# Delta rule: odd heads on exchanged quarters of the rows, solve products on eight array tiles in two banks, per-chunk products ordered over sixteen tiles

## What is computed

```python
def step(S, xs):
    qc, kc, vc, bc = xs
    kb = kc * bc[:, None]
    A = jnp.tril(kb @ kc.T, -1)
    U = solve_triangular(eye + A, vc * bc[:, None] - kb @ S, lower=True)
    o = qc @ S + jnp.tril(qc @ kc.T) @ U
    return (S + kc.T @ U, o)
```

## Time and profile before

| | |
|---|---|
| median of three runs | 824.07 us |
| the profiled execution, span | 869.1 us |
| projecting stage, 17.0 to 113.6 us | 96.6 us, TensorE busy 58.0 |
| delta stage, steps 0 and 1 | 27.0 us, TensorE busy 17.1 |
| delta stage, steps 2 to 15 | 143.6 us, TensorE busy 124.2 |
| all that comes behind 291 us | 578.1 us |

### The profile page before, as it was taken

How to read it: one execution, slowest core, us unless ns; L and a number is a source line. 1 busy time by engine, 2 the same in 40 slices (tenths; PEclk the granted TensorE clock), 3 DMA queues, 4 the chain that set the end, 5 groups by cost and what they waited for, 6 DMA issues and landing times. The chain is left out here.

```text
span 869.1 us, 38511 instructions
## 1 busy us (share of the span) xinstructions
PE 638.0 (73%) x15559; PEld 550.7 (63%) x15559; DVE 388.2 (45%) x1166; ACT 275.3 (32%) x666; POOL 375.3 (43%) x773
## 2 busy tenths in 40 slices
PE   5775457888888585616998368889985269989993
PEld 4564346888888484516988335567664158978992
DVE  3664602222222135661666413445762844456662
ACT  4552211111111121404665133434532023334441
POOL 4574554211110372055888473220100444387675
PEclk9796655555555566856999757889997569999997
DMA  4001231131110470064655110000000556555551
GB/s 124 8 15 32 69 91 40 59 97 49 54 49 34 142 225 1 0 105 144 196 181 171 40 43 23 16 15 4 4 4 2 91 140 203 191 182 184 198 192 38
DMA packets 64818, 75.08 MB, mean 86 GB/s; under 512 B 16048, under 2 KB 42704, under 8 KB 64704
## 3 DMA queue, kind: packets, MB, share of 16 engines
q1 hardware_dynamic: 60384, 64.38, 24.1%
q0 software_dynamic: 4320, 9.18, 4.4%
HBM read 19.83 MB, written 11.24 MB: 36 GB/s over the span
## 5 line engine op out<-in xcount | busy, mean ns | idle before, releaser
L2017 PE MATMUL e_psH<-spare,e_up_w 128*128 x728 | 102.2, 284 | 9.7 <-issue 6.2
L2017 PEld LDWEIGHTS e_psH<-spare,e_up_w 128*128 128x128 f32 x728 | 90.1, 195 | 18.1 <-issue 18.1
L586 POOL TENSOR_TENSOR tb<-tinv,mb 128x128 f32<-128x128 f32 x64 | 24.3, 403 | 116.3 <-PE d_psY L606 110.1
L2082 ACT ACTIVATE e_pre<-e_psH 128x256 f32<-128x256 f32 x91 | 34.6, 382 | 71.1 <-PE e_psH L2017 66.6
L2027 PE MATMUL e_psY<-vb,e_hT 128*128 x364 | 56.0, 276 | 0.2
L1345 ACT ACTIVATE e_hT<-e_psH,e_b 128x128 f32<-128x128 f32 x156 | 44.6, 368 | 27.9 <-PE e_psH L1301 20.1
L2190 DVE SCALAR_TENSOR_TENSOR e_row<-e_psY,e_row 128x128 f32 x91 | 32.0, 351 | 47.9 <-issue 35.8
L1249 POOL DMA_INDIRECT e_row<-xe_dram,e_read_at x39 | 42.8, 1099 | 17.3 <-issue 6.8
L2183 DVE TENSOR_TENSOR e_hT<-e_pre,e_psH 128x256 f32<-128x256 f32 x91 | 37.6, 413 | 25.3 <-ACT e_pre L2082 15.2
L2027 PEld LDWEIGHTS e_psY<-vb,e_hT 128*128 128x128 f32 x364 | 47.9, 192 | 1.0 <-issue 0.9
L1733 DVE TENSOR_TENSOR spare<-l_psA,l_tri 128x512 f32<-128x512 f32 x64 | 39.7, 680 | 14.3 <-PE l_psA L1561 11.8
(11 more groups left out here) (348 smaller groups left out, 1643.4 us busy)
## 6 DMA issues: line engine op xcount, KB each, us to landing
e_up_w<-wac SPq DMA_DIRECT2D x91, 256.0 KB
e_up_w<-wa SPq DMA_DIRECT2D x39, 256.0 KB
xe_dram<-xe SPq DMA_DIRECT2D x2, 2192.0 KB, 15.4
vk_now<-vk SPq DMA_DIRECT2D x16, 192.0 KB, 2.1
kq_now<-kq SPq DMA_DIRECT2D x16, 192.0 KB, 2.3
outs_dram<-spare SPq DMA_DIRECT2D x39, 64.0 KB
r<-in_L_attn_hidden_states SPq DMA_DIRECT2D x8, 256.0 KB, 4.0
gk_now<-gk SPq DMA_DIRECT2D x16, 128.0 KB, 2.1
```

Of the source, the lines that this page charges most:

```text
L2017: mm = nc.tensor.matmul(psH[i % 3][:, f], up_w[i % WDEEP][:, f * P:(f + 1) * P], xT[:, bass.ds(t, 1)].rearrange("p a l -> p (a l)"), start ...
L2082: act.activation(pre[i % 2][:, :, :], psH[i % 3][:, 0:NF], ACT.Silu).then_inc(silu, 1)
```

## The change

- `place(c, h)` gives the quarter of the 128 rows on which chunk c of head h lies after the first run: c for even heads, c+2 (mod 4) for odd ones.
- `first` and `second` write odd heads to the exchanged quarter, `across` reads them from there and writes them back to their own. So a run uses the tiles (c, c) for even and (c, c+2) for odd heads, eight in all. `psY` becomes two banks, even heads in one and odd heads in the other, and takes what `psZ` held beside it; `seat` gives a pair's place in `y0`, `zz` and `uw`.
- `per_chunk` goes over the heads of a sequence for one of the three products before it begins the next, and reads odd heads from the exchanged rows.
- `scores` writes odd heads to exchanged rows as well. For `scale_rows` odd heads are also needed on their own rows, and their keys on exchanged rows: 4 + 4 matmuls per block and pair are added, in the half of the bank that was free.
- `copy_scores` makes three more copies per pair, two of them into the new `gu`, and the copy of the keys out of `kqn` shrinks to the even heads. `u_sb` takes the place of `g_sb`: `mask_scores`, `scale_rows` and the next `scores` wait for the last of the copies.
- `cau4` and `l_tri2` move into the buffer `spare`.

```diff
+def place(c, h):
+    return (c + 2 * (h % 2)) % NC
...
 def scores(g, pair):
...
                             for i in range(2):
+                                at = place(c, i) * CH
                                 rows = slice((2 * pair + i) * CH, (2 * pair + i) * CH + DK)
-                                mm = nc.tensor.matmul(psF[c * CH:(c + 1) * CH, i, k * 2 * CH:(k + 1) * 2 * CH],
+                                mm = nc.tensor.matmul(psF[at:at + CH, i, k * 2 * CH:(k + 1) * 2 * CH],
                                                       kqT[rows, n, 0, c * CH:(c + 1) * CH], kqT[rows, n, :, c * CH:(c + 1) * CH],
                                                       start=True, stop=True)
+                        rows = slice((2 * pair + 1) * CH, (2 * pair + 1) * CH + DK)
+                        for c in range(NC):
+                            at = 4 * 2 * CH + k * 2 * CH
+                            mm = nc.tensor.matmul(psF[c * CH:(c + 1) * CH, 1, at:at + CH],
+                                                  kqT[rows, n, 0, c * CH:(c + 1) * CH], kqT[rows, n, 0, c * CH:(c + 1) * CH],
+                                                  start=True, stop=True)
+                        for c in range(NC):
+                            at, to = 4 * 2 * CH + k * 2 * CH + CH, place(c, 1) * CH
+                            mm = nc.tensor.matmul(psF[to:to + CH, 1, at:at + DK],
+                                                  kqT[rows, n, 0, c * CH:(c + 1) * CH], eye[rows, 0:DK],
+                                                  start=True, stop=True)
...
 def copy_scores(g, pair):
...
-                                   ACT.Copy).then_inc(g_sb, 1)
+                                   ACT.Copy)
+                    if g and pair == 0:
+                        act.wait_ge(a_step, 2 * g)
+                    own_rows = psF[:, :, :].rearrange("p i (u k a l) -> p k i u a l", u=2, k=4, a=2)
+                    for i in range(2):
+                        act.activation(gu[:, :, 2 * pair + i], own_rows[:, :, i, i, 0], ACT.Copy)
+                    act.activation(steps_of(kq, g)[:, :, 2 * pair + 1, 0:DK], own_rows[:, :, 1, 1, 1, 0:DK], ACT.Copy).then_inc(u_sb, 1)
...
-        psY, psZ = bank("d_psY", [P, B * H, RW]), bank("d_psZ", [P, B * H, RW])
+        psY = bank("d_psY", [P, 2, 512])
...
 def apply(i, right, done):
...
-                            mm = nc.tensor.matmul(out[row(c), bh], tb[i][:, bh // H, bh % H].rearrange("p s i -> p (s i)")[row(c)],
+                            mm = nc.tensor.matmul(psY[row(place(c, bh)), bh % 2, y_of(bh)], tb[i][:, bh // H, bh % H].rearrange("p s i -> p (s i)")[row(c)],
                                                   right(bh)[row(c)], start=True, stop=True)
...
 def across(t, start):
...
-                            mm = nc.tensor.matmul(psZ[row(c), bh], gk_now[key(c), bh], y0[key(c), bh * RW:(bh + 1) * RW], start=True, stop=True)
+                            at = key(place(c, bh))
+                            mm = nc.tensor.matmul(psY[row(c), bh % 2, z_of(bh)], gk_now[at, bh], y0[at, seat(bh):seat(bh) + RW], start=True, stop=True)
...
 def per_chunk(t, start):
...
                             for c in range(NC):
-                                nc.tensor.matmul(psC[row(h), c, b * P:b * P + RW], uw[row(c), at + DV:at + DV + CH], kq_now[row(c), bh],
+                                on_row = row(place(c, h))
+                                nc.tensor.matmul(psC[row(h), c, b * P:b * P + RW], uw[on_row, at + DV:at + DV + CH], kq_now[on_row, bh],
                                                  start=True, stop=True)
+                        for h in range(H):
+                            bh, at = b * H + h, seat(b * H + h)
                             for c in range(NC):
...
```

More of the change, by code:

```diff
@@ L309, in scores @@
                     if 2 * g + pair:
-                        pe.wait_ge(g_sb, 2 * g + pair)
+                        pe.wait_ge(u_sb, 2 * g + pair)
                         pe.wait_ge(m_sb, 2 * g + pair)
@@ L324, in _ @@
                 x_up(1)
+                pe.wait_ge(masks, 3)
                 pe.wait_ge(w_in, 16 * 5)
@@ L434, in mask_scores @@
                 def mask_scores(g, pair):
-                    dve.wait_ge(g_sb, 2 * g + pair + 1)
+                    dve.wait_ge(u_sb, 2 * g + pair + 1)
                     for i in range(2):
@@ L549, in key, with seat, y_of, z_of @@
             return slice(c * CH, c * CH + DK)
+        HALF_W = B * H // 2 * RW
         def wide(t):
-            return t[:, 0:B * H * RW].rearrange("p (h c) -> p h c", c=RW)
+            return t[:, 0:2 * HALF_W].rearrange("p (i x) -> p i x", i=2)
+        def seat(bh):
+            return (bh % 2) * HALF_W + bh // 2 * RW
+        def y_of(bh):
+            return slice(bh // 2 * RW, (bh // 2 + 1) * RW)
+        def z_of(bh):
+            return slice(HALF_W + bh // 2 * RW, HALF_W + (bh // 2 + 1) * RW)
         with nc.Block() as block:
@@ L601, in _, with apply @@
             def _(pe):
-                def apply(i, right, out, done):
+                def apply(i, right, done):
                     for bh in range(B * H):
                         for c in range(NC):
-                            mm = nc.tensor.matmul(out[row(c), bh], tb[i][:, bh // H, bh % H].rearrange("p s i -> p (s i)")[row(c)],
+                            mm = nc.tensor.matmul(psY[row(place(c, bh)), bh % 2, y_of(bh)], tb[i][:, bh // H, bh % H].rearrange("p s i -> p (s i)")[row(c)],
                                                   right(bh)[row(c)], start=True, stop=True)
@@ L615, in first @@
                     pe.sem_inc(passed, 1)
-                    apply(0, lambda bh: vk_now[:, bh], psY, y_ps)
+                    apply(0, lambda bh: vk_now[:, bh], y_ps)
                 def across(t, start):
@@ L631, in second @@
                     pe.sem_inc(passed, 1)
-                    apply(1, lambda bh: zz[:, bh * RW:(bh + 1) * RW], psY, w_ps)
+                    apply(1, lambda bh: zz[:, seat(bh):seat(bh) + RW], w_ps)
                 def per_chunk(t, start):
@@ L644, in per_chunk @@
                         for h in range(H):
[L645 removed]
+                            bh, at = b * H + h, seat(b * H + h)
                             for c in range(NC):
[L647 removed]
+                                on_row = row(place(c, h))
+                                nc.tensor.matmul(psC[row(h), c, b * P:b * P + RW], uw[on_row, at + DV:at + DV + CH], kq_now[on_row, bh],
                                                  start=True, stop=True)
+                        for h in range(H):
+                            bh, at = b * H + h, seat(b * H + h)
                             for c in range(NC):
[L650 removed]
+                                on_row = row(place(c, h))
+                                nc.tensor.matmul(psC[row(h), c, b * P + RW + CH:b * P + RW + 2 * CH], uw[on_row, at:at + DV], kq_now[on_row, bh, DK:RW],
                                                  start=True, stop=True)
+                        for h in range(H):
+                            bh, at = b * H + h, seat(b * H + h)
                             for c in range(NC):
[L653 removed]
+                                on_row = row(place(c, h))
+                                mm = nc.tensor.matmul(psC[row(h), c, b * P + RW:b * P + RW + CH], kq_now[on_row, bh, 0:CH], uw[on_row, at:at + DV],
                                                       start=True, stop=True)
```

24 lines of the change are left out of this document (11 added, 13 removed).

## The result

The changed kernel takes **839.92 us** (median of four runs, 838.50 to 842.51) against 824.29 for the kernel before on the same chip: ratio 1.0181, 95% interval [1.0138, 1.0224]. It is slower by 15.6 us where 19 less were forecast, and outside the range. Of 25 later runs of the kernel before, 14 took 820 to 831 us and 11 took 840 to 853; the ratios of this document are formed with the quicker kind alone, and the execution of 869.1 us that the prediction read the earlier trace rows is longer than all of them.

The account below looks back on a forecast made before the run. Bound taken: each delta step is a serial chain through TensorE at clock 0.50. Delta stage -27.4 us plus projecting stage +8.4 gives -19.0, so 824.07 becomes 805 us; forecast 797 to 814 (68%), range 792 to 820.

Parts of the forecast that it names:

- The three solve runs: Delta stage: first, across and second, on eight tiles, fall from 1.50 to 0.97 us each, saving 1.59 us per step.
- The per-chunk products: End of each delta step: the new order over sixteen tiles shortens 2.62 us of records, saving 0.25 us.
- The steps: Delta stage: 1.84 us saved in each of fourteen steps, 25.8 us, plus 1.6 in the first step: -27.4 us.
- the signs that the prediction set itself: Right: runs 0.9-1.06 us, products 2.0-2.62, step 8.2-8.7, delta start 5-14 later, clock 0.50; wrong: projecting stage over 14 longer.
- Rival (b): Instruction issue is the bound: per-chunk products gain nothing, projecting stage pays all 14 us; 818 us, chance 13%.
- (a): Tiles sharing rows take turns: solve runs stay 1.50 us, products 2.62, projecting stage still pays 8.4; 832.5 us, chance 8%.
- (d): The change doesn't do what it says, odd heads landing on the old tiles; would end like (a), chance 2%.
- Rival (c): Denser runs raise the delta stage's granted clock from 0.50 to 1.00; about 792 us, chance 9%.
- -27.4 + 8.4 = -19.0 us: Whole kernel: delta stage gain plus projecting stage cost, worked out in the 869.1 us profile, applied to the 824.07 us median.
- 1.0 for instruction fetch: Projecting stage: loading 2,048 more TensorE instructions costs 1.0 us, a part of the +8.4 us.
- The chain of one group: Projecting stage: added copies and score matmuls lengthen one group's chain from first copy to next activation by 1.65 us.
- what of it would hide: Projecting stage: slack of 1.5 us per early group and inversion steps hide part of the delay, leaving +8.4 us with fetch.

Follow-up runs that it names:

- b2: The kernel before, unchanged, profiled a third time after the prediction: 847.88 us.
- b1: The kernel before, unchanged, profiled again; of its new profiles the nearest to the median: 821.88 us.
- g1: The changed kernel's delta stage with the old projecting stage; SP's loads of each step exchange the odd heads' halves: 825.45 us, ratio 1.0010.
- e7: e5 with one matmul of 96 columns in place of each eight small added ones, 256 extra instructions instead of 2,048: 850.19 us.
- e5: e4 with the added score matmuls kept but the three extra copies per pair removed: 836.25 us.
- e4: The change with every head on its own quarter: solve runs on four tiles, added matmuls and copies kept: 849.23 us, ratio 1.024.
- e6: e4 with the three extra copies per pair kept but the added score matmuls removed: 838.28 us.
- e2: The change with the per-chunk products in the old order, head by head: 845.17 us, ratio 1.0197.
- g2: g1 with the per-chunk products in the old order: 826.84 us, ratio 1.0012.
- the fill: The change plus one unread 128x128x128 matmul in each of three waiting places of a step, steps 1 to 15: 851.70 us, ratio 1.0303.
- b0: The kernel before, unchanged, profiled again for the first time after the prediction: 831.71 us, ratio 1.0042.

## Why the prediction was wrong

**The three solve runs: right.** 0.97 us was forecast for a run at 0.50, 1.01 was measured; its records start 11.6 ns apart (0.73 us from first to last) where 11.0 was taken from the scores. **The per-chunk products: right**: 2.62 - 2.29 = 0.33 us, forecast 0.25. **The steps**: 8.45 us, forecast 10.26 - 1.84 = 8.42. At equal clock the stage goes from 174.1 (174.9 in b2) to 147.3, -26.8, and -27.4 was forecast. Of the signs that the prediction set itself, the run (1.01), the products (2.29), the step (8.45) and the clock (0.51) came out as right; the delta stage begins 18 us later, which it had named as a sign of being wrong. Rival (b) falls, for the records of the products do come faster: 10.7 ns apart and not 12.5. Rivals (a) and (d) fall, for a run takes 1.01 us and not 1.50. "TensorE: Matmul & The Clock Gate", Part 3 (The mechanism), of the Trainium skill says that weight loads overlap matmuls in flight only when their groups of rows differ; the prediction's reading of it, that tiles on the same rows take turns, does not agree with these 1.01 us. Rival (c) falls too: the clock did not rise.

**"-27.4 + 8.4 = -19.0 us: 850.1 in the profile's own time; 824.07 - 19.0 = 805.1": this step failed.** It carries a difference that was worked out at a clock of 0.50 over to executions that have another, as its opening says ("I work in the profile's microseconds and apply the difference to the median"). The prediction saw that the profile was 5.5% long and did not ask in which stages the 45 us lay. Against b1, which is 49 us shorter, they are 21.8 us of the delta stage, 22.2 of the attention stage and 3.6 of closing and norm. The gain in the delta stage against b1 is 5.0 us, so **22 us of the forecast gain were in time that the median does not contain.** That is most of the 34.6 us between -19.0 and the measured +15.6; the projecting stage, +18.1 where +8.4 was forecast, makes 9.7 more. g1, which has this delta stage without the longer projecting stage, bears it out: it gains nothing over the kernel before.

The rows at hand could have priced that. The records of a run of four tiles start 19.4 ns apart at 0.50; if a tile is held half as long at 1.00, that is 9.7 ns, and the earlier trace rows give 9.4 for eight tiles at 1.00. At full clock, by this estimate, the change is worth almost nothing. Measured: 10.8 ns for four tiles (b1) and 9.4 for eight (after, near 245 us), a run of 0.88 us against one of 0.79. A rival "the timed runs have the delta stage at a higher clock", with a gain between none and 27 us, was missing; (c) asked only whether the change would raise the clock.

**"1.0 for instruction fetch (2,048 more TensorE instructions)": mis-sized.** e7 against e5 makes it 8.5 us, and the waits on issue inside the stage add up to 8.4 in the changed kernel (9.5 in e5, 5.7 in e4). The earlier trace rows had the price: stalls of 0.89 and 1.63 us in the delta stage's straight code, with seven packets in 27 us. Eight more packets in the projecting stage are several such stalls, not one.

**The chain of one group: right; what of it would hide: too much.** 1.65 us per group was forecast from the first copy on. ScalarE's timeline after, beside the earlier trace rows:

```profile
69.44 0.38 ACT L379 ACTIVATE gk<-psF 128x256 f32<-128x256 f32 x1
69.72 0.44 ACT L385 ACTIVATE gu<-psF 128x128 f32<-128x128 f32 x2
70.03 0.24 ACT L386 ACTIVATE kq<-psF 128x64 f32<-128x64 f32 x1
...
72.67 0.38 ACT L379 ACTIVATE gk<-psF 128x256 f32<-128x256 f32 x1 [1.74 <-PE psF L335]
72.95 0.44 ACT L385 ACTIVATE gu<-psF 128x128 f32<-128x128 f32 x2
73.27 0.25 ACT L386 ACTIVATE kq<-psF 128x64 f32<-128x64 f32 x1
73.37 0.65 ACT L396 ACTIVATE hT<-conv 128x512 f32<-128x512 f32 x1
```

From the first copy to the next activation it is 73.37 - 69.44 = 3.93 us, and was 63.44 - 61.12 = 2.32: 1.61 more. With the loading taken off, 18.1 - 8.5 = 9.6 us remain for eight groups, 1.2 of 1.6 each, where 7.4 were forecast. Alone, the copies cost 2.7 us (e6) and the longer TensorE runs 3.5 (e7), so in each alone much did hide; no run shows where the remaining 3.4 us come from.

In one line: forecast -27.4 + 8.4; measured against b1 -5.0 + 18.1, and some 5 us in stages that the change does not touch.

**What stays open** is why the clock rises in the delta stage of the kernel before and hardly in that of the change. g1 rules out the longer projecting stage, e2 and g2 show that the order moves it by 0.07 only, and the fill shows that the share of time with a matmul in flight is not it. e4 comes nearest: it differs from the change by one line, which puts the solve runs back on four tiles, and its four runs have mean clocks of 0.775 to 0.801 where those of the change have 0.762 to 0.767. So the lower clock comes with the solve runs on eight tiles; whether it does so because they are shorter, no run has shown. The profiles agree with it: the five with eight tiles have 0.50 to 0.58 in the delta stage, of the nine with four tiles seven have 0.56 to 0.74 and two 0.50. Over whole executions the mean clock was 0.762 to 0.775 in the twelve of g1, and 0.806 to 0.822 in the 14 of the kernel before that took 820 to 831 us.

## What to carry to other kernels

Before a gain is worked out in a profile, set its stages beside the median: where the profiled execution is longer, find the stages that may hold the difference, and price each term at both clock levels. Count the instructions of straight code as work: 2,048 instructions (512 small matmuls) cost 8.5 us here that no engine's busy time shows, and 64 long matmuls with about as much TensorE time did not. Three timed runs that agree do not say how far executions lie apart: here it was 26 us. Where operands must be rearranged, a load that runs anyway may do it almost for nothing: three transfers in place of one, on a queue with room, did the job of 512 matmuls and 48 copies, and the delta stage was 1.9 us longer.

## What was not expected of the hardware

- The granted clock of one and the same program differs by execution in one stage: 0.50, 0.65 and 0.72 in the delta stages of b2, b0 and b1, with 22 us between them.
- Eight tiles gain little from the clock: their records start 11.6 ns apart at 0.50 and 9.4 at 1.00; those of four tiles 19.5 and 10.8.
- Three full-array matmuls in a step, 0.80 us of records each, put where TensorE otherwise waits for a copy or the subtraction, lengthened the step by 1.25 us.
- Waits of 0.4 to 2.1 us in the middle of TensorE's runs ended 2.1 to 3.0 us after a 16 KB packet of instructions began to load, in all 30 cases.
- A transfer of SP's queue took 0.60 to 0.64 us in g1, where three or four follow one another, and 0.47 in the kernel before, where they stand alone. It is not that half the rows cost more: the whole `vk_now` took 0.62 in g1 as well.
